# Normalised rows on GpSimd with statistics two slots ahead, and a reworked order in the gates' stage

## The chip, the cores and the metric

One core of one Trainium2 chip runs the whole program. The metric is the device time of one execution in microseconds. Matmuls run on TensorE (PE), element work on VectorE (DVE), ScalarE (ACT) and GpSimd (POOL). All DMAs of this kernel are issued by one queue, SyncE (SP).

## What is computed

For each of 64 graphs with 256 nodes and 256 features, two layers are applied (cut from the reference):

```python
# layer 0
h = max(layernorm(x), 0)
# in the GNN, on h:
x_conv = relu(bn(conv1d(relu(bn(conv1d_1x1(h))), 17 taps)) + h)
s = h @ w_se.T + b_se;  A = exp(-|s_n - s_m|^2) * adj
x_nmp = A @ relu(h @ w_msg.T + b_msg)
gi = concat(x_conv, x_nmp) @ w_ih.T + b_ih;  gh = h @ w_hh.T + b_hh
r = sigmoid(gi_r + gh_r);  z = sigmoid(gi_z + gh_z)
n = tanh(gi_n + r * gh_n)
x = x + (1 - z) * n + z * h
# layer 1
h2 = max(layernorm(x), 0)
x = x + relu(h2 @ W[:d] + (adj @ h2) @ W[d:] + bias)
```

## The kernel before, in words

The program has four stages, one after the other.

1. **Weights** (up to about 77 us): the filters of the long convolution are transformed and split into two f16 halves.
2. **Convolution stage** (about 77 to 390 us), `convolution`. A loop over slots q = 0 to 65 is written out in the program. Slot q has turn(q) (four transposes of the normalised rows xhat), conv1(q-1), forward(q-2) (the transform into frequencies) on PE, and from slot 18 on three chunks of three "main" matmuls each (the products in frequency space). The layer norm of graph f is made in three steps. `layer_stats(f)` takes mean and variance (two `bn_stats` and two `bn_aggr` on DVE, from `xin`). `layer_rstd(f)` makes the root on POOL. `normalise(f)` makes xhat from `xin`, two `tensor_scalar` of 128 x 256 values each, in the kernel before on DVE. xhat and `xin` have two buffers each, by f % 2.
3. **Rest of the main products** (about 390 to 564 us), 60 units of 12 matmuls.
4. **Gates' stage** (about 564 us to the end), `gates`. A slot t has, on each engine, steps of graph t ("cur"), of graph t-1 ("prev") and of graph t+1 ("nxt"), in an order written by hand. Slots 2 to 61 run in a hardware loop of two slots.

Engines synchronise by semaphores only, and each engine does its own instructions strictly in program order, so that a wait holds all that is behind it on its engine. On the SP queue of the convolution stage, slot q issues in this order: `load_x`, `load_adj(q)`, `store_filters(q)` (only in slots 0 to 11), `store_xhat(q)`, `store_h(q)`, then stores of bins and of y. Four waits matter for what follows:

- `load_x(f)` overwrites `xin[f % 2]`, so it waits for `xhat_done` to reach f-1, that is, for normalise(f-2);
- `store_xhat(f)` waits for normalise(f);
- `normalise(f)` overwrites `xhat[f % 2]`, so it waits for turn(f-2) (`turned`) and for store_xhat(f-2) to have landed (`xhat_stored`);
- `turn(f)` on PE waits for normalise(f).

In the gates' stage, `weighted` (PE, into ps_b) is read by `weighted_high` (ACT, L1638) and then `weighted_low` (DVE, L1643), which releases `gates_second(0)` on PE (semaphore `nmp_low`). `gate_sums` (DVE, L1687 and L1690) reads ps_rz and ps_n when `gates_second` is done, and frees ps_n for the next `first_h`. `adj_split_low` is L1578. `finish` (L1817 and L1821) makes the result of a graph from ps_l, which `neighbours` filled.

## Time and profile before

| | |
|---|---|
| median of 3 runs | 1869.83 us (1867.81 to 1880.15) |
| profiled execution | 1870.98 us, of which the span of instructions is 1868.8 us |
| busy share | PE 95%, DVE 80%, ACT 47%, POOL 24% |
| mean granted clock of TensorE | 0.992 of full speed |
| DMA | 245.56 MB, 131 GB/s over the span |

The profiled execution is 1.15 us above the median. Its span is the time from the first to the last instruction, and 2.2 us lie around it. Busy shares are means over stages with different limits, and the rows below are read by stage.

### The profile page before, as it was taken

How to read it: one execution, taken by the hardware profiler on the slowest of the kernel's cores; microseconds unless marked ns; L12 is line 12 of the kernel's file. 1: busy time of each engine (PE TensorE's matmuls, PEld its weight loads, DVE VectorE, ACT ScalarE, POOL GpSimd, SP SyncE). 2: the span in 40 equal slices, each digit the busy share in tenths (PEclk: the TensorE clock that was granted, in tenths of full speed). 3: DMA queues.
4: the chain of work that ended last, by engine and by line, in shares of the span. 5: the costliest groups of instructions: out<-in, count | busy, mean ns of one | idle time of the engine just before them, and what ended most of it. 6: DMA issues, size and time to landing. Idle time of an engine off the chain costs nothing.

```text
span 1868.8 us, 36896 instructions
## 1 busy us (share of the span) xinstructions
PE 1768.8 (95%) x12477; PEld 1167.3 (62%) x12478; DVE 1495.5 (80%) x3322; ACT 875.8 (47%) x1617; POOL 439.2 (24%) x616
## 2 busy tenths in 40 slices
PE   3768999999998999999999999999999999999996
PEld 1456777764445666666666666666666666666664
DVE  4899999962346888888888888888888888888886
ACT  3675555553344444444444444444444444444442
POOL 4511111101012222222222222222222232222221
PEclk9899999999999999999999999999999999999999
DMA  6298887767732322322322322322322322322320
GB/s 201 98 331 261 303 295 270 265 224 250 253 132 94 104 76 81 102 78 80 101 79 80 100 80 79 100 81 78 99 83 76 99 84 75 100 85 74 101 86 17
DMA packets 175187, 245.56 MB, mean 131 GB/s; under 512 B 14781, under 2 KB 111028, under 8 KB 174635
## 3 DMA queue, kind: packets, MB, share of 16 engines
q1 hardware_dynamic: 175128, 244.81, 39.9%
q8 instruction: 33, 0.54, 0.1%
q14 instruction: 26, 0.20, 0.0%
HBM read 154.57 MB, written 90.18 MB: 131 GB/s over the span
## 4 chain that ended last, share of the span: by engine, by line
PE 40%; DVE 21%; ACT 5%; issue 3%; DVEq 0%; POOL 0%; POOLq 0%
PE ps_rz L1551 18%; PE ps_l L1551 13%; PE ps_n L1551 7%; ACT big L1696 3%; ACT big L1591 3%; DVE big L1687 2%; DVE big L1586 2%; DVE big L1621 2%; DVE big L1643 2%; DVE big L1595 2%; DVE big L1578 2%; DVE big L1730 2%; DVE big L1704 2%; PE ps_d L1765 2%; DVE big L1734 2%
## 5 line engine op out<-in xcount | busy, mean ns | idle before, releaser
L1551 PE MATMUL ps_rz<-big 128*128 128x512 f16 x2304 | 560.6, 379 | 13.0 <-DVE big L1643 10.7
L1551 PEld LDWEIGHTS ps_rz<-big 128*128 128x128 f16 x2304 | 220.0, 98 | 224.0 <-DVE big L1643 20.0
L1551 PE MATMUL ps_n<-big 128*128 128x256 f16 x2304 | 314.2, 273 | 0.0
L1551 PEld LDWEIGHTS ps_n<-big 128*128 128x128 f16 x2304 | 225.3, 98 | 94.5
L1551 PE MATMUL ps_l<-big 128*128 128x512 f16 (+1 forms) x1536 | 271.9, 327 | 2.9 <-DVE big L1800 1.5
L1264 PE MATMUL m_ps<-big 128*128 128x512 f16 (+1 forms) x1152 | 268.3, 375 | 3.0 <-DVE big L1029 2.2
L1721 POOL TENSOR_TENSOR big<-big 128x256 f32<-128x256 f32 x128 | 97.5, 762 | 666.9 <-ACT big L1714 666.9
L1696 ACT ACTIVATE big<-big,w_scale 128x512 f32<-128x512 f32 x128 | 92.0, 719 | 283.3 <-DVE big L1687 283.3
L1551 PEld LDWEIGHTS ps_l<-big 128*128 128x128 f16 x1536 | 149.9, 98 | 90.9 <-DVE big L1800 2.0
L1551 PE MATMUL ps_b<-big 128*128 128x256 f16 x1536 | 188.6, 272 | 1.5 <-DVE big L1621 1.5
L1264 PEld LDWEIGHTS m_ps<-big 128*128 128x128 f16 x1152 | 111.8, 98 | 105.1 <-issue 2.2
L1551 PEld LDWEIGHTS ps_b<-big 128*128 128x128 f16 x1536 | 147.0, 98 | 36.3 <-DVE big L1621 19.9
L1034 DVE SCALAR_TENSOR_TENSOR ysb<-m_ps,ysb 128x512 f16<-128x512 f32 x96 | 66.1, 689 | 97.8 <-ACT ysb L926 97.5
L1687 DVE TENSOR_TENSOR big<-ps_rz,w_bias_rz 128x512 f32<-128x512 f32 x128 | 88.8, 693 | 41.5 <-PE ps_rz L1551 36.7
L1714 ACT ACTIVATE big<-big,w_scale 128x256 f32<-128x256 f32 x128 | 65.4, 511 | 92.2 <-DVE big L1707 92.2
L926 ACT ACTIVATE ysb<-m_ps 128x512 f16<-128x512 f32 x96 | 57.0, 594 | 92.5 <-PE m_ps L1264 83.2
L1223 PE MATMUL c_ps<-w1t,front 128*128 128x259 f16 x768 | 97.9, 278 | 0.0
L1817 DVE SCALAR_TENSOR_TENSOR big<-ps_l,w_scale,w_bias_out 128x256 f32<-128x256 f32 x128 | 61.7, 482 | 45.1 <-PE ps_l L1551 45.1
L904 ACT ACTIVATE front<-c 128x512 f16<-128x512 f32 x64 | 40.4, 631 | 121.5 <-DVE c L1017 121.5
L1638 ACT ACTIVATE big<-ps_b 128x512 f16<-128x512 f32 x64 | 38.5, 601 | 124.6 <-PE ps_b L1551 124.6
L1772 ACT ACTIVATE big<-ps_d 128x512 f16<-128x512 f32 x64 | 38.3, 598 | 114.1 <-PE ps_d L1765 114.1
L1521 ACT ACTIVATE big<-ps_s,cvec 128x256 f32<-128x256 f32 x128 | 65.3, 560 | 54.6 <-PE ps_s L1510 54.6
(242 smaller groups left out, 2892.7 us busy)
## 6 DMA issues: line engine op xcount, KB each, us to landing
spectra<-ysb SPq DMA_DIRECT2D x96, 256.0 KB, 2.4
big<-spectra SPq DMA_DIRECT2D x64, 384.0 KB, 3.5
xin<-in_x SPq DMA_DIRECT2D x64, 256.0 KB, 4.0
x_normed<-front SPq DMA_DIRECT2D x64, 256.0 KB, 4.3
h_turned<-front SPq DMA_DIRECT2D x64, 256.0 KB, 3.9
big<-h_turned SPq DMA_DIRECT2D x64, 256.0 KB, 3.2
big<-in_adj SPq DMA_DIRECT2D x64, 256.0 KB, 3.6
big<-in_x SPq DMA_DIRECT2D x64, 256.0 KB, 2.8
```

Source lines behind the costliest of these rows:

```text
L926: act.activation(ysb[:, m % 3, :, 0, :], m_ps[m % 3][:, :].rearrange("p (r o) -> p r o", r=2), ACT.Copy, scale=2.0 ** Y_EXP).then_inc(y_hi ...
L1034: dve.scalar_tensor_tensor(out=ysb[:, m % 3, :, 1, :], in0=m_ps[m % 3][:, :].rearrange("p (r o) -> p r o", r=2), scalar=2.0 ** Y_EXP, in1= ...
L1223: last = pe.matmul(c1_ps[:, t, 0:D + SE], ht[:, f % 2, dl, kh, t * P:t * P + P], w1t[:, wl, kh, 0:D + SE], start=(kh == 0 and n == 0), sto ...
L1264: last = pe.matmul(dest, x_, w_, start=n == 0, stop=n == 11, skip_group_check=True)
L1521: act.activation(conv_y[:, oh, :], ps_s[:, oh * N:oh * N + N], ACT.Identity, scale=cvec[:, 4 + oh:5 + oh], bias=cvec[:, 6 + oh:7 + oh]).th ...
L1551: last = pe.matmul(dest, stationary(dl), moving(wl), start=start and n == 0, stop=stop and n == 2, **kw)
L1591: act.activation(att_s[:, 0, :, :], att[:, :, :], ACT.Copy, scale=w["scale"][:, 6:7]).then_inc(S["att_high"], 1)
L1687: dve.tensor_tensor(sum_rz[:, i, :], ps_rz[i][:, :], w["bias_rz"][:, :], ALU.add).then_inc(S["rz_added"], 1)
L1696: act.activation(tanh_rz[:, i, :], sum_rz[:, i, :], ACT.Tanh, scale=w["scale"][:, 8:9]).then_inc(S["rz_tanh"], 1)
L1714: act.activation(new[:, i, :], pre_n[:, i, :], ACT.Tanh, scale=w["scale"][:, 10:11]).then_inc(S["n_tanh"], 1)
L1721: pool.tensor_tensor(x_new[:, i, :], xin[:, p, i, :], new[:, i, :], ALU.add).then_inc(S["x_new_done"], 1)
L1817: dve.scalar_tensor_tensor(out=out_sum[:, i, :], in0=ps_l[i][:, 0:D], scalar=w["scale"][:, 11:12], in1=w["bias_out"][:, :], op0=ALU.mult, ...
```

## The change

In the convolution stage `normalise` moves from DVE to POOL, behind `layer_rstd` of the same graph. DVE takes the statistics of graph q+2 in slot q, where it took those of q+1, and waits for `xhat_done` before it overwrites `meanvar`. SP loads x one graph earlier: slot q issues `load_x(q+3)` where it issued `load_x(q+2)`, and `load_x(2)` stands ahead of the loop.

In the gates' stage, PE does `neighbours(t-1)` behind `gates_second(t, 1)` where it stood ahead of it. DVE does `gate_sums(t, 1)` at the end of slot t where it was the first step of slot t+1, `weighted_low` ahead of `adj_split_low`, and the result of a graph one slot later, in pieces (`out_row` twice, then `finish`). An extra slot at the end takes the last graph's result.

```diff
@@ SP, convolution stage @@
+                load_x(2)
                 for q in range(SLOTS):
-                    if q + 2 < graphs:
-                        load_x(q + 2)
+                    if q + 3 < graphs:
+                        load_x(q + 3)
@@ POOL, convolution stage @@
-                layer_rstd(0)
-                for q in range(graphs - 1):
-                    layer_rstd(q + 1)
+                def normalise(f):
+                    pool.wait_ge(rstd_done, f + 1)
+                    if f >= 2:
+                        pool.wait_ge(turned, f - 1)
+                        pool.wait_ge(xhat_stored[f % 2], 16 * (f // 2))
+                    for t in range(H):
+                        last = pool.tensor_scalar(xhat[:, f % 2, t, :], xin[:, f % 2, t, :], meanvar[:, f % 2, t, 0:1],
+                                                  rstd[:, f % 2, t:t + 1], ALU.subtract, ALU.mult)
+                    last.then_inc(xhat_done, 1)
+
+                for f in range(graphs):
+                    layer_rstd(f)
+                    normalise(f)
@@ DVE, convolution stage @@
                     dve.wait_ge(x_loaded[f % 2], 16 * (f // 2 + 1))
+                    if f >= 2:
+                        dve.wait_ge(xhat_done, f - 1)
...
                 layer_stats(0)
-                normalise(0)
+                layer_stats(1)
                 for q in range(SLOTS):
-                    if q + 1 < graphs:
-                        layer_stats(q + 1)
+                    if q + 2 < graphs:
+                        layer_stats(q + 2)
...
-                    if q + 1 < graphs:
-                        normalise(q + 1)
@@ gates' stage: new function, and finish without its first step @@
+        def out_row(dve, t, p, i):
+            ready(dve, "out_done", t, i + 1, H)
+            dve.scalar_tensor_tensor(out=out_sum[:, i, :], in0=ps_l[i][:, 0:D], scalar=w["scale"][:, 11:12],
+                                     in1=w["bias_out"][:, :], op0=ALU.mult,
+                                     op1=ALU.add).then_inc(S["out_added"], 1)
@@ SP, gates' stage @@
-                    if prev:
-                        store(sp, t - 1, 1 - p)
+                    if old:
+                        store(sp, t - 2, p)
@@ PE, gates' stage @@
                         first_conv_n(pe, t, p, 1)
+                    if cur:
+                        gates_second(pe, t, p, 1)
                     if prev:
                         neighbours(pe, t - 1, 1 - p)
-                    if cur:
-                        gates_second(pe, t, p, 1)
```

The order of instructions, at the two places that the prediction speaks of. First, the SP queue at the start of the convolution stage (xin<-in_x is `load_x`, wb<-big `store_filters`, x_normed<-front `store_xhat`, h_turned<-front `store_h`). Before:

```order
L692 DMA xin<-in_x 128x2x256 [waits xhat_done]
L740 DMA w_bias_rz<-in_adj 128x512
L712 DMA wb<-big 128x2048
L696 DMA x_normed<-front 128x512 [waits xhat_done]
L700 DMA h_turned<-front 128x1024 [waits h_low]
```

Now:

```order
L692 DMA xin<-in_x 128x2x256 [waits xhat_done] x2
L740 DMA w_bias_rz<-in_adj 128x512
L712 DMA wb<-big 128x2048
L696 DMA x_normed<-front 128x512 [waits xhat_done]
L700 DMA h_turned<-front 128x1024 [waits h_low]
```

One load of x more is issued first, so from here on each load of x in the queue is that of the next graph, and its wait for `xhat_done` asks for one more normalise, ahead of the same stores. On POOL the root was alone (graphs 0 and 1, before):

```order
L813 MEMSET minus_half 128x2
L814 MEMSET eps 128x2
L819 TENSOR_TENSOR rstd<-meanvar,eps 128x2 [waits stats_done,cleared]
L821 TENSOR_TENSOR rstd<-rstd,minus_half 128x2 [waits var_done]
L819 TENSOR_TENSOR rstd<-meanvar,eps 128x2 [waits stats_done]
```

Now (graphs 1 and 2):

```order
L820 TENSOR_TENSOR rstd<-meanvar,eps 128x2 [waits stats_done]
L822 TENSOR_TENSOR rstd<-rstd,minus_half 128x2 [waits var_done]
L831 TENSOR_SCALAR front<-xin,meanvar,rstd 128x256 [waits rstd_done]
L831 TENSOR_SCALAR front<-xin,meanvar,rstd 128x256
L820 TENSOR_TENSOR rstd<-meanvar,eps 128x2 [waits stats_done]
L822 TENSOR_TENSOR rstd<-rstd,minus_half 128x2 [waits var_done]
L831 TENSOR_SCALAR front<-xin,meanvar,rstd 128x256 [waits xhat_stored0,turned,rstd_done]
L831 TENSOR_SCALAR front<-xin,meanvar,rstd 128x256
```

The two normalising instructions and their wait for the store stand on POOL between the roots of neighbouring graphs. Second, DVE in the gates' loop, from the statistics of graph t-1 to `h2_split_low` (L1754 or L1755 is `norm2`). Before:

```order
L1742 BN_AGGR big<-big 128x2
L1578 SCALAR_TENSOR_TENSOR big<-big,w_scale 128x512 [waits g_adj_high]
L1643 SCALAR_TENSOR_TENSOR big<-ps_b,big 128x512 [waits g_nmp_high]
L1754 TENSOR_SCALAR big<-big 128x256 [waits g_turned2,g_rstd2]
L1754 TENSOR_SCALAR big<-big 128x256
L1466 ISA
L1687 TENSOR_TENSOR big<-ps_rz,w_bias_rz 128x512 [waits g_rz_tanh,g_rz_done]
L1690 TENSOR_TENSOR big<-ps_n,w_bias_n 128x512 [waits g_pre_done,g_n_done]
L1777 SCALAR_TENSOR_TENSOR big<-ps_d,big 128x512 [waits g_h2_high]
```

Now:

```order
L1743 BN_AGGR big<-big 128x2
L1814 SCALAR_TENSOR_TENSOR big<-ps_l,w_scale,w_bias_out 128x256 [waits g_out_done]
L1644 SCALAR_TENSOR_TENSOR big<-ps_b,big 128x512 [waits g_nmp_high]
L1755 TENSOR_SCALAR big<-big 128x256 [waits g_turned2,g_rstd2]
L1755 TENSOR_SCALAR big<-big 128x256
L1579 SCALAR_TENSOR_TENSOR big<-big,w_scale 128x512 [waits g_adj_high]
L1814 SCALAR_TENSOR_TENSOR big<-ps_l,w_scale,w_bias_out 128x256 [waits g_out_done]
L1467 ISA
L1688 TENSOR_TENSOR big<-ps_rz,w_bias_rz 128x512 [waits g_rz_tanh,g_rz_done]
L1691 TENSOR_TENSOR big<-ps_n,w_bias_n 128x512 [waits g_pre_done,g_n_done]
L1778 SCALAR_TENSOR_TENSOR big<-ps_d,big 128x512 [waits g_h2_high]
```

The split of adj went behind `weighted_low` and `norm2`, and the two rows of an older graph's result (ps_l) stand among them.

## Rows read from the trace of the kernel before

**Rows 1.** Windows: stretch, length, busy us of PE, PEld, DVE, ACT, POOL, clock, DMA, GB/s

```profile
130.00:140.00 10.00, 6.86 (x62) 5.86 (x61) 9.40 (x27) 7.29 (x16) 1.77 (x4) 1.00 1.01 335
142.24:155.53 13.29, 9.65 (x84) 8.18 (x84) 13.19 (x37) 7.45 (x19) 2.65 (x6) 1.00 0.77 238
200.00:220.00 20.00, 20.00 (x151) 14.86 (x150) 19.86 (x53) 12.05 (x30) 3.53 (x8) 1.00 0.91 316
800.00:1000.00 200.00, 198.45 (x1439) 131.59 (x1438) 167.00 (x361) 89.50 (x160) 51.05 (x60) 1.00 0.27 87
```

**Rows 2.** Timeline, turn on PE in five slots: start, us, engine, line, op

```profile
137.48 0.66 PE L1212 MATMUL turn_ps<-ident,front 128*128 128x128 f32 x4 [1.57 <-DVE front L1001]
142.26 0.66 PE L1212 MATMUL turn_ps<-ident,front 128*128 128x128 f32 x4 [1.57 <-DVE front L1001]
146.70 0.66 PE L1212 MATMUL turn_ps<-ident,front 128*128 128x128 f32 x4 [1.22 <-DVE front L1001]
...
307.71 0.60 PE L1212 MATMUL turn_ps<-ident,front 128*128 128x128 f32 x4
...
312.65 0.60 PE L1212 MATMUL turn_ps<-ident,front 128*128 128x128 f32 x4
```

**Rows 3.** Line L1212 over the run: ns min/median/max, first and last start

```profile
L1212 PE MATMUL turn_ps<-ident,front x256: 272/273/476, 81.0 to 387.2; 128*128 128x128 f32 x128
```

**Rows 4.** Timeline of the SP queue, three issues back to back

```profile
186.43 0.43 SPq L692 DMA_DIRECT2D xin<-in_x  x1
186.90 0.50 SPq L740 DMA_DIRECT2D w_bias_rz<-in_adj  x1
187.45 0.43 SPq L696 DMA_DIRECT2D x_normed<-front  x1
```

**Rows 5.** Line L696, window 185.5 to 190.5: issue to landing of that one store

```profile
DMA to landing us min/median/max: 3.5/3.5/3.5
```

**Rows 6.** Timeline of the SP queue, first slot, with a store of filters between

```profile
80.90 0.37 SPq L692 DMA_DIRECT2D xin<-in_x  x1
...
82.31 0.43 SPq L696 DMA_DIRECT2D x_normed<-front  x1
```

**Rows 7.** Line L696, window 80.5 to 84: landing of that store

```profile
DMA to landing us min/median/max: 4.4/4.4/4.4
```

**Rows 8.** Line L696, all 64 stores of xhat: issue to landing

```profile
DMA to landing us min/median/max: 3.3/4.3/6.4
```

**Rows 9.** Page, DMA issues: KB each, median us to landing

```profile
spectra<-ysb SPq DMA_DIRECT2D x96, 256.0 KB, 2.4
...
xin<-in_x SPq DMA_DIRECT2D x64, 256.0 KB, 4.0
```

**Rows 10.** POOL instructions of the same size: ns min/median/max, first and last start

```profile
L304 POOL TENSOR_SCALAR big<-big,row_scale x10: 920/926/1219, 25.0 to 50.8; 119x256 f32<-119x256 f32 x10
L1721 POOL TENSOR_TENSOR big<-big x128: 637/877/882, 582.0 to 1851.1; 128x256 f32<-128x256 f32 x128
```

**Rows 11.** Timeline of one gates' slot, PE, ACT and DVE

```profile
1011.10 1.47 PE L1551 MATMUL ps_b<-big 128*128 128x256 f16 x12
...
1012.69 0.60 ACT L1638 ACTIVATE big<-ps_b 128x512 f16<-128x512 f32 x1 [1.95 <-PE ps_b L1551]
...
1012.85 0.72 DVE L1578 SCALAR_TENSOR_TENSOR big<-big,w_scale 128x512 f16<-128x512 f32 x1
...
1013.48 0.69 DVE L1643 SCALAR_TENSOR_TENSOR big<-ps_b,big 128x512 f16<-128x512 f32 x1
...
1014.23 1.47 PE L1551 MATMUL ps_rz<-big 128*128 128x512 f16 x6 [0.16 <-DVE big L1643]
...
1017.46 0.69 DVE L1777 SCALAR_TENSOR_TENSOR big<-ps_d,big 128x512 f16<-128x512 f32 x1 [0.37 <-ACT big L1772]
...
1018.58 2.75 PE L1551 MATMUL ps_l<-big 128*128 128x512 f16 x12
```

**Rows 12.** Timeline, the same ps_rz group one slot later

```profile
1034.28 1.47 PE L1551 MATMUL ps_rz<-big 128*128 128x512 f16 x6 [0.15 <-DVE big L1643]
```

More of the change, by code:

```diff
@@ L993, in layer_stats @@
                     last.then_inc(stats_done, 1)
-                def normalise(f):
-                    dve.wait_ge(rstd_done, f + 1)
-                    if f >= 2:
-                        dve.wait_ge(turned, f - 1)
-                        dve.wait_ge(xhat_stored[f % 2], 16 * (f // 2))
-                    for t in range(H):
-                        last = dve.tensor_scalar(xhat[:, f % 2, t, :], xin[:, f % 2, t, :], meanvar[:, f % 2, t, 0:1],
-                                                 rstd[:, f % 2, t:t + 1], ALU.subtract, ALU.mult)
-                    last.then_inc(xhat_done, 1)
                 def split_h(f):
@@ L1815, in finish @@
             for i in range(H):
-                ready(dve, "out_done", t, i + 1, H)
-                dve.scalar_tensor_tensor(out=out_sum[:, i, :], in0=ps_l[i][:, 0:D], scalar=w["scale"][:, 11:12],
-                                         in1=w["bias_out"][:, :], op0=ALU.mult,
-                                         op1=ALU.add).then_inc(S["out_added"], 1)
                 ready(dve, "out_added", t, i + 1, H)
@@ L1825, in slots @@
         def slots(engine, slot):
-            slot(0, 0, False, True, True)
-            slot(1, 1, True, True, True)
+            slot(0, 0, False, False, True, True)
+            slot(1, 1, False, True, True, True)
             with engine.Fori(1, (graphs - 2) // 2) as j:
                 for p in range(2):
-                    slot(j * 2 + p, p, True, True, True)
-            slot(graphs - 2, 0, True, True, True)
-            slot(graphs - 1, 1, True, True, False)
-            slot(graphs, 0, True, False, False)
+                    slot(j * 2 + p, p, True, True, True, True)
+            slot(graphs - 2, 0, True, True, True, True)
+            slot(graphs - 1, 1, True, True, True, False)
+            slot(graphs, 0, True, True, False, False)
+            slot(graphs + 1, 1, True, False, False, False)
         with nc.Block() as block:
@@ L1840, in _, with slot @@
                     sp.wait_ge(early.y_stored[i], 16 * (2 * HALF_UNITS * graphs // GROUP // 3))
-                def slot(t, p, prev, cur, nxt):
+                def slot(t, p, old, prev, cur, nxt):
                     if nxt:
@@ L1859, in _, with slot @@
                 conv_add(pool, 0, 0)
-                def slot(t, p, prev, cur, nxt):
+                def slot(t, p, old, prev, cur, nxt):
                     if prev:
@@ L1876, in _, with slot @@
                 conv_split_high(act, 0, 0)
-                def slot(t, p, prev, cur, nxt):
+                def slot(t, p, old, prev, cur, nxt):
                     if prev:
@@ L1906, in _, with slot @@
                 conv_split_low(dve, 0, 0)
-                def slot(t, p, prev, cur, nxt):
+                def slot(t, p, old, prev, cur, nxt):
                     if prev:
-                        gate_sums(dve, t - 1, 1 - p, 1)
                         gate_new(dve, t - 1, 1 - p, 1)
@@ L1919, in slot @@
                         x1_stats(dve, t - 1, 1 - p, 1)
+                    if old:
+                        out_row(dve, t - 2, p, 0)
                     if cur:
-                        adj_split_low(dve, t, p)
                         weighted_low(dve, t, p)
@@ L1925, in slot @@
                     if cur:
+                        adj_split_low(dve, t, p)
+                    if old:
+                        out_row(dve, t - 2, p, 1)
+                    if cur:
                         gate_sums(dve, t, p, 0)
@@ L1928, in slot @@
                         h2_split_low(dve, t - 1, 1 - p)
+                    if old:
+                        finish(dve, t - 2, p)
                     if cur:
@@ L1936, in slot @@
                         conv_split_low(dve, t + 1, 1 - p)
-                    if prev:
-                        finish(dve, t - 1, 1 - p)
+                    if cur:
+                        gate_sums(dve, t, p, 1)
                 slots(dve, slot)
@@ L1945, in _, with slot @@
                 inverse(pe, 0, 0)
-                def slot(t, p, prev, cur, nxt):
+                def slot(t, p, old, prev, cur, nxt):
                     if cur:
@@ L1967, in slot @@
                         first_conv_n(pe, t, p, 1)
+                    if cur:
+                        gates_second(pe, t, p, 1)
                     if prev:
                         neighbours(pe, t - 1, 1 - p)
-                    if cur:
-                        gates_second(pe, t, p, 1)
                 slots(pe, slot)
```

## The prediction

> **What bounds the kernel now.** I read the windows by stage first, then the timeline of one slot in each stage, then the SP queue. The convolution stage has two limits. In its first 18 slots (no main products yet) DVE is busy 9.40 of 10 us and PE only 6.86 [rows 1], and each turn on PE comes after an idle time of 1.2 to 1.6 us that the normalising instruction on DVE, L1001, ended [rows 2]. A slot takes 142.26 - 137.48 = 4.78 us with a store of filters in it (slots 0 to 11) and 146.70 - 142.26 = 4.44 us without (12 to 17). In the other slots PE is busy 20.00 of 20 us [rows 1] and a slot takes 312.65 - 307.71 = 4.94 us [rows 2]: DVE is nearly as full (19.86) but PE sets the pace. The gates' stage is bound by PE too, 198.45 of 200 us [rows 1], with a slot of 1034.28 - 1014.23 = 20.05 us and one small stall in it, 0.15 to 0.16 us for L1643 on DVE [rows 11, 12].
>
> **The convolution stage: what is removed.** DVE loses two L1001 per slot. In the PE-bound slots that frees an engine that isn't the bound and gives nothing. In the first 18 slots it could give at most the work removed, about 0.73 us of DVE per slot, 18 x 0.73 = 13 us. That is the gain if nothing else comes in its way.
>
> **The convolution stage: the new chain.** Something does. Follow the queue. normalise(q+2) on POOL waits until store_xhat(q) has landed. store_xhat(q) is issued by SP in slot q, behind load_x, and load_x is now that of graph q+3, which waits for normalise(q+1). So the chain is: normalise(q+1) ends, SP issues load_x(q+3), load_adj(q), in slots 0 to 11 store_filters(q), then store_xhat(q); this lands; normalise(q+2) runs. One turn of this ring is one slot. In the kernel before, load_x(q+2) asked only for normalise(q), so store_xhat(q) could go out one normalise earlier and the same ring had two slots of time, about 9.6 to 9.9 us. The store of xhat(q) itself has been ready for a whole slot when SP at last comes to it. Queued behind the waiting load on SP are load_adj, both stores and the stores of bins and y; behind the waiting normalise on POOL is the next root; PE waits for all of it at turn(q+2).
>
> The period of the ring, step by step:
> - POOL's end to SP's issue: 0.05 us, an estimate from L1001's ends and the next L692 in the timeline.
> - From the issue of load_x to that of store_xhat: 187.45 - 186.43 = 1.02 us when the three go out back to back [rows 4], and 82.31 - 80.90 = 1.41 us with a store of filters between [rows 6].
> - Issue to landing of the store: 3.5 us in just that burst [rows 5], 4.4 us in the burst with filters [rows 7]. Over all 64 stores it is 3.3 to 6.4 with median 4.3 us [rows 8]. I take the two bursts, because the ring makes exactly these.
> - Landing to POOL's start: 0.05 us, an estimate of the same kind.
> - normalise on POOL: the trace has no such instruction with two scalar operands. The nearest is L304, a TENSOR_SCALAR with one scalar operand, 119 x 256 f32, median 926 ns; L1721 of 128 x 256 with two tensors takes 637 to 882 ns [rows 10]. I take 2 x 0.93 and 0.14 for the second operation and the gap, 2.0 us. The bounds are 2 x 0.64 + 0.07 = 1.35 and 2 x 1.22 + 0.1 = 2.54 us.
>
> Sum: 0.05 + 1.02 + 3.5 + 0.05 + 2.0 = 6.62 us in a slot without filters, 0.05 + 1.41 + 4.4 + 0.05 + 2.0 = 7.91 us with. Nothing else is later. The load of x(q+2) is issued after normalise(q), lands 4.0 us later [rows 9], and statistics (1.05 us) and root (0.96 us) follow; that is ready before normalise(q+1) has ended one ring later, so it hides. PE's own 4.94 us of work per slot hides in 6.62 as well.
>
> turn(0) starts at 81.0 [rows 3]. normalise(0) takes 1.3 us longer on POOL, so turn(0) moves to about 82.4, and turn(1), behind a root (0.96) and a normalise (2.0) on POOL, comes at about 85.5. Then there are 62 turns of the ring, 12 with filters and 50 without: 12 x 7.91 + 50 x 6.62 = 94.9 + 331.0 = 425.9 us, and turn(63) comes at 511.4 us where the last one starts at 387 now [rows 3]. **This costs +124 us.** What lies behind it in the stage is unchanged.
>
> A rule on the DMA's price can be set beside this. The row shows 3.5 us [rows 5]. The Trainium skill (DMA: Bandwidth & Descriptors, Anatomy of one DMA) gives about 2.0 us fixed and the bytes at 436 GB/s; as an estimate from that page a 256 KB store would land in 2.6 us, the rings would be 5.7 and 6.1 us, and the cost about +75 us. The measured row decides for me; the page's fit leaves out the two loads that share the engines.
>
> **The gates' stage.** L1643 starts at 1013.48, though ACT's half was ready at 1012.69 + 0.60 = 1013.29, because L1578 stands in front of it and runs from 1012.85 [rows 11]. With the split of adj behind it, it can start at about 1013.32, 0.16 us sooner, which is all of PE's stall; ACT sets the end then. 62 slots x 0.16 = 10 us. The out_row in front of it has room: the statistics end 0.5 us before ACT does. gates_second(1) comes 1.3 us earlier on PE than its reader needs, which only adds slack at ps_n, and neighbours needs its input 1.95 us later; at the very end it takes about 1 us off the drain. **-11 us.** What DVE does later in the slot grows by the moved pieces: L1777 ends at 1018.15, while PE starts layer1 at 1018.58 [rows 11], so there is 0.4 us of room, and with out_row and the split of adj (0.48 + 0.72 us) ahead of gate_sums this room is nearly used, since DVE idled about as long there. I cost it at nothing; if it is overrun by 0.2 us, the gain is gone and no more.
>
> **The sum.** 1870.98 + 124 - 11 = 1984 us for the profiled execution, 1983 us against the median.
>
> **Rivals.**
> 1. *The ring holds, at another price* (the forecast's own spread). With the shortest landing of 3.3 us [rows 8] and 1.35 us of POOL the periods are 5.77 and 6.16 us: 74 + 289 = 363 us, 61 us more than now, total about 1922. With the medians that the loaded queue shows (4.3, 4.7 with filters) and 2.54 us of POOL they are 7.96 and 8.75 us: 503 us, total about 2061.
> 2. *The ring does not bind, and the change is faster.* The ring must turn in 4.94 us. With 1.02 us of issues, 1.35 us of POOL and the hops this needs a landing of 2.4 us, which is what a store of y with nothing in front of it takes [rows 9]; with my 2.0 us it needs 1.8. Then DVE's 13 us and the gates' 11 us are gained: 1847 us. Against it: no xhat store of 64 landed under 3.3 us [rows 8], and two loads stand directly in front of it.
> 3. *POOL is held off by DVE.* L1721 of one shape takes 637 ns in some slots and 877 in most [rows 10]. If each normalising instruction meets such an overlap with L1022, the ring grows by 2 x 0.24 us, 62 x 0.48 = 30 us: about 2014 us. If a whole L1022 of 0.69 us blocks each normalise it is 43 us, 2027. The Trainium skill (SBUF — State Buffer, Who interferes with whom) says that a DVE instruction with two SBUF inputs contends with a GpSimd instruction that reads SBUF. By that rule L1022, which reads two SBUF tensors, would be the one to meet here.
> 4. *TensorE's clock falls.* PE would be busy about 4.94 of 6.62 us, 75%. In 142 to 155 us it is busy 9.65 of 13.29 us, 73%, at a granted clock of 1.00 [rows 1], which speaks against it. If it did fall to 1.2 GHz for good, the work of 50 slots would take 9.9 us each: +165 us, about 2150.
>
> **Chances.** The ring at a price between 1930 and 2050 us, rival 3 included: 0.84. Cheaper, 1860 to 1930: 0.05. Dearer or the clock: 0.08. Rival 2: 0.03. A measurement of this kernel can tell about 1%. Faster by over 1% 0.03, within 1% 0.01, slower 0.96. The predicted time is 1983 us, the range 1930 to 2050.
>
> **What the new profile would show.** Right: turns spaced by 6 to 8 us over the whole convolution stage, PE idle before L1212 with POOL's normalise as releaser, POOL waiting for the DMA x_normed<-front, DVE idle too, a gates' slot of 19.9 us. Wrong at the ring: turns still 4.9 us apart. Wrong at a price: the landing of L696 or the mean of the POOL TENSOR_SCALAR off 3.5 us and 1.0 us. Wrong at the gates: a wait of PE for gate_sums or h2_split_low in place of L1643.

## The result and the profile after

The changed kernel takes 2042.24 us (median of 4 runs, 2041.09 to 2045.48), the kernel before 1869.3 us beside it. The ratio is 1.0922 with a 95% interval of 1.0887 to 1.0956: 173 us slower. That is 59 us above the forecast of 1983 us and 8 us inside the upper end of its range. The profiled execution took 2045.48 us with a span of 2043.7 us. The lines of the changed kernel lie a little further down than before: turn on PE is L1213 (L1212 before), the normalising instruction is L831 and now on POOL (L1001 on DVE before), the second half of split_h1 on DVE is L1025 (L1022 before), the four SP issues are L692 (load_x), L740 (load_adj), L712 (store_filters) and L696 (store_xhat) as before.

The loss is in the convolution stage. Line L1213 over the run, on PE alone without its weight loads (instruction durations in ns, first and last start, then what ended PE's idle time before it, in us and times), answers to [rows 3]:

```profile
L1213 PE MATMUL turn_ps<-ident,front x256: 272/273/477, 80.5 to 572.2; 128*128 128x128 f32 x128
its engine sat idle before it (us, times) until:
  POOL front L831: 157.2, 58
```

The last turn starts at 572.2 us where it started at 387.2 before: 185 us later. The windows of one piece of that stage and one of the gates' stage (same columns as [rows 1]):

```profile
100.00:120.00 20.00, 10.72 (x56) 8.02 (x56) 7.92 (x21) 7.26 (x16) 8.11 (x9) 0.74 0.43 158
300.00:350.00 50.00, 36.72 (x240) 24.52 (x238) 29.09 (x73) 18.74 (x43) 23.69 (x26) 0.93 0.51 180
800.00:1000.00 200.00, 200.00 (x1450) 133.09 (x1448) 164.79 (x362) 89.95 (x161) 49.66 (x62) 1.00 0.28 87
```

Around 300 us PE is busy 36.72 of 50 us, DVE 29.09, POOL 23.69 and the DMA engines half: no resource is full. That is what a chain of latencies looks like. In the gates' stage PE is now busy 200.00 of 200 us, 198.45 before [rows 1].

The timeline of POOL, of SP's issues and of turn on PE shows the chain, two turns of it:

```profile
305.58 0.39 SPq L692 DMA_DIRECT2D xin<-in_x  x1
...
306.53 0.43 SPq L696 DMA_DIRECT2D x_normed<-front  x1
...
310.09 2.95 POOL L831 TENSOR_SCALAR front<-xin,meanvar,rstd 128x256 f32<-128x256 f32 x2 [3.58 <-DMA x_normed<-front]
...
313.07 0.39 SPq L692 DMA_DIRECT2D xin<-in_x  x1
...
313.10 0.66 PE L1213 MATMUL turn_ps<-ident,front 128*128 128x128 f32 x4 [0.66 <-POOL front L831]
...
314.02 0.43 SPq L696 DMA_DIRECT2D x_normed<-front  x1
...
317.84 2.76 POOL L831 TENSOR_SCALAR front<-xin,meanvar,rstd 128x256 f32<-128x256 f32 x2 [3.84 <-DMA x_normed<-front]
...
320.63 0.39 SPq L692 DMA_DIRECT2D xin<-in_x  x1
```

Read it as a ring. POOL's normalisation ends at 313.04, SP issues load_x at 313.07 and store_xhat at 314.02, the store lands and POOL starts again at 317.84. From load_x to load_x it is 7.49 and 7.56 us, and PE starts turn 0.06 us after POOL's end (313.10). With a store of filters between, the same timeline reads:

```profile
130.38 0.39 SPq L692 DMA_DIRECT2D xin<-in_x  x1
...
130.40 1.11 PE L1213 MATMUL turn_ps<-ident,front 128*128 128x128 f32 x4 [3.76 <-POOL front L831]
...
131.80 0.43 SPq L696 DMA_DIRECT2D x_normed<-front  x1
...
136.26 2.72 POOL L831 TENSOR_SCALAR front<-xin,meanvar,rstd 128x256 f32<-128x256 f32 x2 [4.96 <-DMA x_normed<-front]
...
139.01 0.39 SPq L692 DMA_DIRECT2D xin<-in_x  x1
```

8.63 us. Over the whole run, first the POOL line, with what it waited for, and then the landing of its stores (this answers to [rows 8]):

```profile
L831 POOL TENSOR_SCALAR front<-xin,meanvar,rstd x128: 1216/1227/1770, 77.9 to 569.1; 128x256 f32<-128x256 f32 x128
its engine sat idle before it (us, times) until:
  DMA x_normed<-front: 260.5, 61
```

```profile
DMA to landing us min/median/max: 3.2/3.6/6.1
```

So 61 of the 62 waits of POOL for the buffer of the store two graphs before are real, 260.5 us in all.

In the gates' stage the timeline of one slot shows what became of the stall of [rows 11]:

```profile
1214.52 0.60 ACT L1639 ACTIVATE big<-ps_b 128x512 f16<-128x512 f32 x1 [2.67 <-PE ps_b L1552]
...
1215.15 0.69 DVE L1644 SCALAR_TENSOR_TENSOR big<-ps_b,big 128x512 f16<-128x512 f32 x1 [0.80 <-ACT big L1639]
...
1215.90 1.47 PE L1552 MATMUL ps_rz<-big 128*128 128x512 f16 x6
```

L1644 now waits for ACT and not for DVE's own queue, and PE has no idle time before ps_rz. Over all slots, the ps_rz line of the page, before and then now (busy us, mean ns, then PE's idle time before it):

```profile
L1551 PE MATMUL ps_rz<-big 128*128 128x512 f16 x2304 | 560.6, 379 | 13.0 <-DVE big L1643 10.7
```

```profile
L1552 PE MATMUL ps_rz<-big 128*128 128x512 f16 x2304 | 560.6, 379 | 1.9 <-DVE big L1545 1.1
```

13.0 us of idle time became 1.9.

### The profile page after: what moved, and what is told of

It reads as the page before. It is cut to its first block, busy times and chain, and to the rows that moved or that the text cites. A ratio compares the mean times of both kernels' runs of the same rounds, so it can differ in the third digit from the quotient of the medians.

```text
span 2043.7 us, 37050 instructions
## 1 busy us (share of the span) xinstructions
PE 1830.8 (90%) x12478; PEld 1196.0 (59%) x12478; DVE 1437.3 (70%) x3194; ACT 879.4 (43%) x1617; POOL 592.8 (29%) x744
## 4 chain that ended last, share of the span: by engine, by line
PE 62%; DVE 1%; ACT 0%; issue 0%; POOL 0%; POOLq 0%; DVEq 0%
PE ps_rz L1552 24%; PE ps_l L1552 12%; PE ps_n L1552 12%; PE ps_b L1552 8%; PE ps_s L1511 3%; PE ps_d L1766 1%; PE ps_d L1561 1%; ACT big L1697 0%; DVE big L1688 0%; DVE big L1705 0%; DVE big L1731 0%; ACT big L1592 0%; DVE big L1587 0%; DVE big L1622 0%; DVE big L1596 0%
## 5 line engine op out<-in xcount | busy, mean ns | idle before, releaser
L1265 PE MATMUL m_ps<-big 128*128 128x512 f16 (+1 forms) x1152 | 277.4, 383 | 1.2 <-DVE ysb L1037 0.6
L1722 POOL TENSOR_TENSOR big<-big 128x256 f32<-128x256 f32 x128 | 105.3, 823 | 590.7 <-ACT big L1715 590.7
L831 POOL TENSOR_SCALAR front<-xin,meanvar,rstd 128x256 f32<-128x256 f32 x128 | 170.4, 1340 | 260.9 <-DMA x_normed<-front 260.5
L1213 PE MATMUL turn_ps<-ident,front 128*128 128x128 f32 x256 | 51.7, 336 | 160.8 <-POOL front L831 157.2
L1002 DVE BATCH_NORM_STATS2 stats<-xin 128x6 f32<-128x256 f32 x128 | 48.1, 418 | 188.6 <-DMA xin<-in_x 188.3
L1213 PEld LDWEIGHTS turn_ps<-ident,front 128*128 128x128 f32 x256 | 33.4, 166 | 186.9 <-POOL front L831 175.5
L1224 PE MATMUL c_ps<-w1t,front 128*128 128x259 f16 x768 | 129.0, 333 | 0.0
L1224 PEld LDWEIGHTS c_ps<-w1t,front 128*128 128x128 f16 x768 | 91.9, 120 | 37.0 <-issue 5.8
L1528 POOL TENSOR_TENSOR big<-big 128x512 f32<-128x512 f32 x64 | 74.3, 1162 | 134.1 <-ACT big L1522 131.4
```

What stands on the lines that cost most here:

```text
L831: last = pool.tensor_scalar(xhat[:, f % 2, t, :], xin[:, f % 2, t, :], meanvar[:, f % 2, t, 0:1], rstd[:, f % 2, t:t + 1], ALU.subtract, A ...
L1002: dve.bn_stats(stats[:, f % 2, t, :], xin[:, f % 2, t, :]).then_inc(stats_raw, 1)
L1213: last = pe.transpose(turn_ps[:, kh * N + t * P:kh * N + t * P + P], xhat[:, f % 2, t, kh * P:kh * P + P], ident[:, :])
L1224: last = pe.matmul(c1_ps[:, t, 0:D + SE], ht[:, f % 2, dl, kh, t * P:t * P + P], w1t[:, wl, kh, 0:D + SE], start=(kh == 0 and n == 0), sto ...
L1265: last = pe.matmul(dest, x_, w_, start=n == 0, stop=n == 11, skip_group_check=True)
L1528: pool.tensor_tensor(conv_x[:, :, :], conv_y[:, :, :], ht[:, p, 0, :, :], ALU.add).then_inc(S["conv_h"], 1)
```

## The experiments

Ten kernels, two of them measured twice. Names: q is the slot, f or q+1, q+2 the graph. Diffs are against the changed kernel if nothing else is said.

### Each part alone

The convolution stage as changed, the gates' stage as before (only the core of the diff; + is this kernel):

```diff
-                    if old:
-                        store(sp, t - 2, p)
+                    if prev:
+                        store(sp, t - 1, 1 - p)
...
+                        gate_sums(dve, t - 1, 1 - p, 1)
...
+                        adj_split_low(dve, t, p)
...
-                        adj_split_low(dve, t, p)
-                    if old:
-                        out_row(dve, t - 2, p, 1)
```

> The convolution stage as changed, the gates' stage as before. Ring theory (each slot of the convolution stage is one turn of: load of x, store of xhat, landing, normalise on GpSimd): the last turn stays at about 572 us and the whole is 10 us above the changed kernel, about 2052 us. A theory in which the gates' reorder costs part of the loss (through a new wait) gives less than 2042 us here.

The gates' stage as changed, the convolution stage as before:

```diff
-                layer_stats(1)
+                normalise(0)
...
-                    if q + 2 < graphs:
-                        layer_stats(q + 2)
+                    if q + 1 < graphs:
+                        layer_stats(q + 1)
...
+                    if q + 1 < graphs:
+                        normalise(q + 1)
```

> The gates' stage as changed, the convolution stage as before. If the reorder removes the 0.16 us stall of each slot and nothing else, 1869 - 10 = 1859 us, with a slot of 19.90 us where it was 20.05. If the stall is only moved to another wait, 1869 us. If the new steps on VectorE hold PE, above 1870.

Measured: the convolution part alone 2052.19 us (ratio 1.0973, 1.0938 to 1.1009), the gates' part alone 1857.91 us (0.9931, 0.9905 to 0.9958). The gates' part takes 2052.19 - 2042.24 = 10.0 us off the one and 1869.8 - 1857.9 = 11.9 off the other (1869.8 is the kernel before, measured beside it). The four runs of the first kernel lie between 2048.3 and 2055.8 us, so within the spread the parts add. Between 800 and 1000 us PE is busy 200.00 of 200 us with the gates' part alone.

What follows: the two parts are independent, the loss is the convolution stage's alone, and the gates' part does what the trace of before promised.

### The ring opened: the store ahead of the load

In SP's order store_xhat(q) is put in front of load_x(q+3), so that it doesn't wait for normalise(q+1). Nothing else changes.

```diff
+                    if q < graphs:
+                        store_xhat(q)
                     if q + 3 < graphs:
                         load_x(q + 3)
...
-                        store_xhat(q)
```

> The changed kernel with one edit: in each slot the SP queue issues store_xhat(q) ahead of load_x(q+3), not behind it. GpSimd still normalises, statistics are still two slots ahead. Ring theory: the store no longer waits for normalise(q+1), the ring has two slots of time again, PE-bound slots go back to 4.94 us and the whole to 1847 to 1862 us. Rival, GpSimd's normalise (2.66 us where VectorE took 0.73) is too slow by itself: the time stays above 2000 us. Rival, TensorE's clock: the same time as the ring theory if its idle time goes, so this run does not tell these two apart.

Measured: 1868.56 us, ratio 0.9988 (0.9971 to 1.0006), 7 us above the range that I had expected. Line L1214 is turn here, on PE alone again:

```profile
L1214 PE MATMUL turn_ps<-ident,front x256: 272/273/448, 81.6 to 395.1; 128*128 128x128 f32 x128
its engine sat idle before it (us, times) until:
...
  POOL front L832: 8.0, 2
```

What follows: POOL ends 8.0 us of PE's waits where it ended 157.2. One issue in another place gives back 2042.24 - 1868.56 = 174 of the 184 us that lie between the changed kernel and the gates' part alone (1857.91 us), with the same slow normalisation on POOL. So nearly the whole loss is the place of the store in SP's queue. It is not quite all: this kernel stays 11 us above the gates' part alone, clear of noise (the intervals 0.9971 to 1.0006 and 0.9905 to 0.9958 don't meet), and POOL still waits 48.3 us in all for stores here. What these 11 us are made of I haven't taken apart.

### The ring opened: a third buffer

The order of SP stays as changed; xhat has three buffers, so that normalise(q+2) waits for store_xhat(q-1), which was issued a whole slot before.

```diff
-                    if f >= 2:
-                        pool.wait_ge(turned, f - 1)
-                        pool.wait_ge(xhat_stored[f % 2], 16 * (f // 2))
+                    if f >= 3:
+                        pool.wait_ge(turned, f - 2)
+                        pool.wait_ge(xhat_stored[f % 3], 16 * (f // 3))
```

> The changed kernel with three buffers of xhat in place of two, SP's order untouched. normalise(q+2) then waits for the landing of store_xhat(q-1), which is one slot older. Ring theory: the ring has two slots and no longer binds; as in the run with the store first, about 1866 us, and 1855 to 1862 if the extra distance also frees the first 18 slots. Rival, SP's order costs by something other than this wait (the queue's other stores held behind the load): above 1900 us.

Measured: 1863.41 us, ratio 0.9967 (0.995 to 0.9985). A second measurement of this kernel, beside others below, gave 1861.36 us; there POOL's line waits 5.3 us in all for stores (260.5 before):

```profile
  DMA x_normed<-front: 4.3, 8
  DMA x_normed<-xhat_c: 1.0, 2
```

What follows: a rival to the ring, that the loads and stores simply take too long for the DMA engines in this order, falls. The landing of the stores is as long as in the changed kernel (median 3.6 us in this second measurement too), it only has time now.

### Each term of the ring

**POOL's duration.** The two normalising instructions back on DVE (0.73 us the pair in place of 2.43 to 2.95), the look-ahead, the loads and SP's order as changed:

```diff
 in the program of DVE
+                    if q + 1 < graphs:
+                        normalise(q + 1)
 in the program of POOL
-                    normalise(f)
```

> The changed kernel with normalise back on VectorE at its old place, statistics and the load of x still one graph further ahead. Theory that the order on SP makes the ring: it still turns once per slot, with VectorE's 0.74 us in place of 2.66: 0.05 + 0.95 + 3.7 + 0.05 + 0.74 = 5.5 us without filters and 6.7 with, about 1910 us; where the next statistics on VectorE wait for x (issued after the same normalise, landing 2.8 us, then 2.7 us of statistics, split and bias ahead of the next normalise) up to 6.5 us per slot and 1965 us. Theory that GpSimd's slow normalise is the loss: with VectorE's normalise the time is that of the gates' part alone, 1858 us.

Measured: 1938.56 us, ratio 1.0352 (1.0321 to 1.0384). Turn goes from 85.4 to 469.7 us, 6.1 us per slot. The theory that POOL's slowness alone makes the loss gave 1858 and is refuted: with DVE's fast instruction the kernel is still 69 us slower than the one before. The ring with DVE would be, from the timings above, 0.95 + 3.5 + 0.73 + 0.1 = 5.3 us, an estimate; the slots take 6.1. The trace of one turn of it:

```profile
304.83 0.43 SPq L696 DMA_DIRECT2D x_normed<-front  x1
...
309.39 0.73 DVE L1003 TENSOR_SCALAR front<-xin,meanvar,rstd 128x256 f32<-128x256 f32 x2
```

The store lands after 3.5 us by the median, 308.3, and DVE comes to its instruction at 309.39 with no idle time before it. What DVE waited for between 80 and 475 us (us in total, times, longest):

```profile
DVE stats L991 <- DMA xin<-in_x: 66.9, 62, 3.3
DVE front L1003 <- DMA x_normed<-front: 15.0, 16, 2.2
```

So the ring of the store is seldom the last to be ready here. What DVE waits for in all 62 slots is the load of x, which SP issues only after the same normalisation: load, statistics, then DVE's other steps, and the next normalisation behind them. It is the second chain that the expectation names. This run refutes the theory of POOL's price alone; it doesn't measure the ring of the store with a fast normalisation.

**The same duration the other way.** A third normalising instruction per graph, into a tile that nothing reads, in front of the two:

```diff
+                    pool.wait_ge(spare_done, f)
+                    pool.tensor_scalar(spare[:, :], xin[:, f % 2, 1, :], meanvar[:, f % 2, 1, 0:1],
+                                       rstd[:, f % 2, 1:2], ALU.subtract, ALU.mult).then_inc(spare_done, 1)
```

> The changed kernel with a third tensor_scalar of 128 x 256 per graph on GpSimd, into a spare tile that nothing reads, between the wait for the store and the two normalising ones. Ring theory: each of 62 turns grows by the instruction's 1.23 to 1.34 us, 76 to 83 us in all, about 2121 us. Rival, GpSimd has slack (it waits 260 us for the store): the instruction hides and the time stays 2042 us.

Measured: 2124.2 us, ratio 1.1356 (1.1324 to 1.1389), 82.0 us over the changed kernel, as expected. In the timeline:

```profile
309.79 1.23 POOL L833 TENSOR_SCALAR spare<-xin,meanvar,rstd 128x256 f32<-128x256 f32 x1 [4.83 <-DMA x_normed<-front]
...
311.00 2.43 POOL L836 TENSOR_SCALAR front<-xin,meanvar,rstd 128x256 f32<-128x256 f32 x2
```

What follows: the extra instruction takes 1.21 us from start to start in this slot and 1.29 us by the mean of all 64, and the time grows by 82.0 / 62 = 1.32 us per turn of the ring. POOL's duration is in the ring at full weight. POOL is busy under half of the time in the changed kernel (23.69 of 50 us), so this is no full engine.

**The issues ahead of the store.** store_xhat(q) directly behind load_x(q+3), ahead of load_adj and the store of filters:

```diff
                     if q + 3 < graphs:
                         load_x(q + 3)
+                    if q < graphs:
+                        store_xhat(q)
...
-                        store_xhat(q)
```

> The changed kernel with store_xhat(q) directly behind load_x(q+3), ahead of load_adj and store_filters. Ring theory: the ring stays but is shorter by the issue of load_adj (0.47 us) and in 12 slots of the filters (0.49 us), and the store lands some 0.3 us sooner with one load less in front of it: 62 x 0.77 + 12 x 1.0 = 60 us less, about 1982 us; at least 62 x 0.47 + 6 = 35 us less, 2007 us. Rival, the ring is not set by the store: no change from 2042 us.

Measured: 1950.09 us, ratio 1.0434 (1.0398 to 1.047). It gave 92 us where I had expected 35 to 60. The rows, POOL's line and then the landing:

```profile
L832 POOL TENSOR_SCALAR front<-xin,meanvar,rstd x128: 1216/1226/1231, 77.2 to 473.9; 128x256 f32<-128x256 f32 x128
its engine sat idle before it (us, times) until:
  DMA x_normed<-front: 166.6, 61
```

```profile
DMA to landing us min/median/max: 2.5/3.1/5.4
```

Three things shrank, of which I had counted one and a half. The issue of the store comes 0.43 us behind load_x and not 0.95 or 1.42: 50 x 0.52 + 12 x 0.99 = 38 us. With one transfer fewer in front of it the store lands sooner. From its issue to POOL's start it is 3.5 us by the mean, where the changed kernel has 4.0 without filters and 4.9 with them: 50 x 0.53 + 12 x 1.39 = 43 us. And no POOL instruction takes over 1231 ns where some took 1770: 2.43 for the pair against a mean of 170.4 / 64 = 2.66 us, 62 x 0.23 = 14 us. The pair still overlaps DVE's split_h1 in most slots, but that one now starts 1.7 to 2.3 us into it (why this matters is said with rival 3 below). Sum 95 us; the two profiled executions differ by 2045.48 - 1948.62 = 97, the medians by 92.

### Is the look-ahead needed at all?

POOL normalises, but statistics and load_x run one slot ahead only, as in the kernel before:

```diff
-                layer_stats(1)
...
-                    if q + 2 < graphs:
-                        layer_stats(q + 2)
+                    if q + 1 < graphs:
+                        layer_stats(q + 1)
...
-                    if q + 3 < graphs:
-                        load_x(q + 3)
+                    if q + 2 < graphs:
+                        load_x(q + 2)
```

> The changed kernel, but statistics and the load of x at their old distance (statistics of q+1 and load of q+2 in slot q); GpSimd normalises. Ring theory: the wait of the load ahead of the store is for normalise(q) again, two slots per ring: slots of 4.94 us in the main part, about 4.6 us in the first 18 (statistics, root, normalise, turn and split now follow each other), the whole 1855 to 1865 us. Rival, GpSimd's normalise is what costs: above 2000 us, since it has even less time here.

Measured: 1901.29 us, ratio 1.0166 (1.0135 to 1.0197). My expectation of 1855 to 1865 us missed by 36 us. The load is issued early enough here, and the ring of the store isn't the bound; another chain is:

```profile
300.67 0.74 DVE L1001 BATCH_NORM_STATS2 stats<-xin 128x6 f32<-128x256 f32 x2
...
301.78 0.20 POOL L819 TENSOR_TENSOR rstd<-meanvar,eps 128x2 f32<-128x2 f32 x1 [2.23 <-DVE meanvar L1004]
...
302.87 2.93 POOL L830 TENSOR_SCALAR front<-xin,meanvar,rstd 128x256 f32<-128x256 f32 x2
...
305.86 0.66 PE L1211 MATMUL turn_ps<-ident,front 128*128 128x128 f32 x4 [0.68 <-POOL front L830]
```

From the statistics to turn it is 305.86 - 300.67 = 5.19 us, all in one slot, and the slot of PE is 4.94 us. PE waits for POOL 56.5 us in all, and POOL for stores only 1.9. That this chain sets the slots is read off the trace; no run here shortens it. Beside the two kernels with the look-ahead and an open ring (1868.6 and 1863.4 us), the look-ahead is worth 33 to 38 us to a kernel that normalises on POOL. The same look-ahead closes the ring when load_x stays ahead of the store in SP's queue. Each half of the change needs something of the other.

### What would the relief of DVE have been worth?

With the ring opened (three buffers) the convolution stage is no faster than before. A cycle of ACT and DVE seemed the cause in the first 18 slots. It can be seen in the kernel with three buffers, by ACT's timeline, with a negation (L949, slots 1 to 11) and without. It negates factors of the convolution's filters, which the first expectation below calls adjacency factors:

```profile
108.72 0.63 ACT L921 ACTIVATE front<-c 128x512 f16<-128x512 f32 x1 [1.35 <-DVE c L1026]
...
110.61 1.06 ACT L949 ACTIVATE big<-big 128x1024 f16<-128x1024 f16 x1
111.56 0.60 ACT L914 ACTIVATE front<-turn_ps 128x512 f16<-128x512 f32 x1
...
113.51 0.63 ACT L921 ACTIVATE front<-c 128x512 f16<-128x512 f32 x1 [1.36 <-DVE c L1026]
...
151.67 0.63 ACT L921 ACTIVATE front<-c 128x512 f16<-128x512 f32 x1 [1.95 <-DVE c L1026]
...
156.11 0.63 ACT L921 ACTIVATE front<-c 128x512 f16<-128x512 f32 x1 [1.95 <-DVE c L1026]
```

4.79 us with, 4.44 us without: the very periods of the kernel before, 4.78 and 4.44 [rows 2], although DVE has 0.73 us less to do. ACT's split_h1 (L921) waits for DVE's add_bias (L1026), which stands behind DVE's split_h, which needs ACT's split_h (L914), which stands behind the negation. Two kernels move the negation from slots 1 to 11 to slots 12 to 22, one with three buffers and POOL's normalisation, one with the gates' part alone (DVE normalises):

```diff
-                    if 1 <= q < HALF_UNITS:
-                        negate(q)
+                    if HALF_UNITS <= q < 2 * HALF_UNITS - 1:
+                        negate(q - HALF_UNITS + 1)
```

> The kernel with three x_hat buffers, with ScalarE's negation of the adjacency factors moved from the units 1 to 11 to the units 12 to 22. In the kernel with three buffers the first 12 units take 4.79 us each, and the next six, which have no negation, 4.44 us. Theory, a cycle of ScalarE and VectorE (split_h, add_bias, split_h1, split_x, adj_sum, negate, split_h of the next unit) sets those units and the negation lies in it: the units 1 to 11 fall to between 4.1 and 4.5 us, the units 12 to 17 rise to about 4.8, and from unit 18 on TensorE hides it. 11 units x 0.35 = 3.9 us won, 5 or 6 x 0.35 = 2 us given back: 1859 to 1862 us, where the same kernel without the move has 1863. Rival, the load of filters or VectorE's own 18 us per 20 us sets them: units of 4.79 us stay and the time is 1863 to 1866.

> The gates' part alone, with ScalarE's negation moved from the units 1 to 11 to the units 12 to 22; the convolution stage normalises on VectorE as before. If the cycle of ScalarE and VectorE sets the first units, the same 0 to 4 us are won: 1854 to 1858 us against 1858 for the gates' part alone. If VectorE's own work sets them (two normalisations more on it, 0.73 us per unit), nothing changes: 1857 to 1860 us. A gain here as large as in the kernel with three buffers says that VectorE's load is not what sets these units.

And the two kernels that they come from, measured again beside them:

> The gates' part alone a second time, beside the two kernels with the moved negation on the same chip: 1858 us, within 3 us of its first measurement (1857.9), so 0.6% under the kernel before.

> The kernel with three x_hat buffers and GpSimd's normalisation a second time, beside the gates' part alone on the same chip. Theory, the normalisation on GpSimd buys nothing even with the ring of the stores taken away, because VectorE was not what set any unit of the convolution stage: the two agree within 6 us (1858 to 1866). Rival, VectorE's relief of 0.73 us per unit shows in the units 0 to 17 once the store is out of the way: 10 us or more under the gates' part alone, 1848 us or less.

| kernel | us (median) | ratio to before (95%) |
|---|---|---|
| gates' part alone, again | 1858.35 | 0.9924 (0.9903 to 0.9946) |
| gates' part, negation later | 1860.85 | 0.9933 (0.9912 to 0.9955) |
| three buffers, again | 1861.36 | 0.9940 (0.9919 to 0.9961) |
| three buffers, negation later | 1865.61 | 0.9977 (0.9960 to 0.9994) |

The moved negation gains nothing in time. Both medians lie above the ranges of the cycle theory (1854 to 1858 and 1859 to 1862 us), and with three buffers the move costs 4 us. 1865.61 lies in the rival's range, but not for the rival's reason, since its slots did change. The periods of the slots did what the cycle says, in turn on PE in the gates' part with the negation later:

```profile
106.62 0.66 PE L1212 MATMUL turn_ps<-ident,front 128*128 128x128 f32 x4 [1.22 <-DVE front L1001]
...
111.05 0.66 PE L1212 MATMUL turn_ps<-ident,front 128*128 128x128 f32 x4 [1.22 <-DVE front L1001]
```

4.43 us, with the store of filters in these slots and with DVE busy 43.19 of 44 us between 106 and 150, where the same slots take 4.79 us with the negation. So the negation sets the difference between 4.79 and 4.44 us; the store of filters doesn't. It is paid back behind. Over the eleven slots from the third turn on this kernel wins 52.68 - 49.34 = 3.3 us on its parent; over the next five, which now have the negation, it loses 23.92 - 22.17 = 1.75 us, and in the slot behind them, which takes 6.79 and not 5.16 us, another 1.6. The six slots behind that lose 30.83 - 29.56 = 1.3 more, though PE bounds them in the parent. In the kernel with three buffers the early slots fell to 4.43 only now and then and came mostly between 4.6 and 5.2, at a DMA share of 0.95 to 0.97. What sets those I haven't separated.

POOL's normalisation buys nothing when nothing stands in its way: 1861.36 against 1858.35 us, intervals overlapping. Turn runs from 80.1 to 386.9 in the one and from 80.6 to 386.7 in the other. In the slots without negation the windows of the two read, DVE's normalisation first and then POOL's:

```profile
140.00:160.00 20.00, 13.55 (x119) 11.49 (x119) 19.86 (x55) 11.29 (x28) 3.94 (x9) 1.00 0.79 246
```

```profile
140.00:160.00 20.00, 15.42 (x124) 11.58 (x124) 17.32 (x47) 11.25 (x26) 14.77 (x19) 1.00 0.70 242
```

DVE falls from 19.86 to 17.32 us of 20, and the slots take 4.43 us in both. In the slots that PE bounds there was nothing to win from the start.

## Why the prediction was right, and where its sizes were off

**The ring: right.** The mechanism came as worked out: turns 7.5 to 8.6 us apart in the rows above, PE waiting for POOL's line, POOL for the store, SP's load directly behind POOL. Two experiments that open it by different means (another order, another buffer) give back 174 and 179 of the 184 us that the convolution part costs, and one that lengthens it by 1.29 us per turn costs 1.32.

**Its price: 61 us too low.** I had put turn(1) at 85.5 and turn(63) at 511.4; they start at 84.9 and 571.9. The mean period is (571.9 - 84.9) / 62 = 7.86 us and not 6.87. By terms, from the timeline of all stores:

- Issue of load_x to issue of store_xhat: 0.95 and 1.42 us against 1.02 and 1.41 predicted. About 4 us less in all.
- The store's landing, issue to POOL's start: mean 4.0 us in the slots without filters (3.4 to 5.5) and 4.9 with them (4.7 without the first, which has two loads in front of it), against 3.55 and 4.45. 49 x 0.45 + 12 x 0.42 = 27 us more. I had taken one burst of each kind for the typical one. The median of 3.6 us agrees with the burst; a sum needs the mean, and of the first 61 stores 18 took 4.5 us or more.
- The normalisation on POOL: mean 170.4 / 64 = 2.66 us the pair against 2.0. 62 x 0.66 = 41 us more, the largest miss. I had taken the instruction with one scalar operand, 926 ns [rows 10]. With two it takes 1227 ns by the median, near the upper end that I had kept (1219, which was the longest of that row).

27 + 41 - 4 = 64 us. The last turn gives back 1.6, since its store has no load in front of it and it takes 5.0 us, and the earlier start 0.6. That makes 62, and the profiled execution is 61 us above the forecast (2045.48 against 1984). **The terms that failed are these two sizes; the step was right.** Both misses went the same way, so that the time lies only 8 us inside the range: the mechanism is confirmed, the price less so.

**Rival 3, POOL held off by DVE, came in part.** What decides is where DVE's L1025 starts. Two slots, the POOL pair of the first being the one at 310.09 above:

```profile
311.34 0.69 DVE L1025 SCALAR_TENSOR_TENSOR front<-c,front 128x512 f16<-128x512 f32 x1 [0.62 <-ACT front L915]
```

```profile
241.78 2.43 POOL L831 TENSOR_SCALAR front<-xin,meanvar,rstd 128x256 f32<-128x256 f32 x2 [3.67 <-DMA x_normed<-front]
...
243.41 0.69 DVE L1025 SCALAR_TENSOR_TENSOR front<-c,front 128x512 f16<-128x512 f32 x1 [0.63 <-ACT front L915]
```

Both times L1025 lies inside the pair. In the first it starts 1.25 us into it, just as the second POOL instruction is due (1.21), and the pair takes 2.95 us. In the second it starts 1.63 us into it and the pair keeps its 2.43. The same pattern runs through all 64 slots. In 35 of them one of the two POOL instructions is due while L1025 runs, or at most 0.12 us before its start, and the pair takes 2.54 to 2.97 us. In 11 L1025 starts 0.15 to 0.26 us after a POOL instruction, and L1025 itself takes 0.82 to 0.94 us while the pair keeps 2.43. In the other 18, 12 of them with an overlap, neither grows. The mean of 2.66 makes 0.23 us per turn, 14 us in all, where I had named 30 to 43. The Trainium skill (SBUF — State Buffer, Who interferes with whom) calls the port that GpSimd shares with VectorE an exclusive lock, and says that a VectorE instruction with two SBUF inputs contends there with a GpSimd instruction that reads SBUF. The trace agrees on which instruction it is, and on POOL's being held back by a running L1025 for most of what is left of it, up to 0.54 us of its 0.69. It differs the other way round: an L1025 that starts 0.4 us or more into a running POOL instruction isn't held back at all.

**The price of the store.** The row of before won over the page's fit, and the measurement is further off still. The Trainium skill (DMA: Bandwidth & Descriptors, Anatomy of one DMA) gives a fit from which 2.6 us is worked out for this store alone, an estimate. The section is about DMAs that GpSimd issues, and this one is issued by SyncE. Here the shortest of 64 takes 3.2 us and the median 3.6, and with one load fewer in front of it the shortest takes 2.5. The prediction's cost by that fit is also summed wrongly: rings of 5.72 and 6.11 us make 50 x 5.72 + 12 x 6.11 = 359 us, which is +58 us on the old stage and not +75.

**Rival 2, and the 13 us of DVE in it: wrong.** This part of my working never came to decide the sum, but it stood there as a gain. Opened, the ring leaves 1861 to 1869 us, not 1847. The step "at most the work removed, 0.73 us of DVE per slot" took DVE's 9.40 of 10 us [rows 1] for the limit. The cycle of ACT and DVE has the same period with 0.73 us less on DVE. That it is this cycle is shown for its one part, the negation, and argued for the rest. The prediction names the slots of 4.78 us by the store of filters; it is the negation in the same slots that makes the difference to 4.44.

**Rival 4, the clock: came, and cost nothing that can be seen.** I had argued that it would stay at 1.00. It was granted at 0.74 between 100 and 120 us and at 0.93 between 300 and 350, means between its two levels of 1.2 GHz (0.5) and 2.4 GHz (1.00), with PE busy 54% and 73% of the time. The row that I had argued from, 73% busy at 1.00 [rows 1], doesn't carry over to a stage with waits of up to 3.8 us (the rows above). Turn takes 1.11 us and not 0.66 in some slots. But PE isn't in the ring: it waits for POOL and no step of the ring waits for it.

**The gates' stage: right in place and size.** -11 us predicted; 10.0, 11.9 and 11.8 us measured (1870.19 - 1858.35 the last). PE's idle time before ps_rz fell by 13.0 - 1.9 = 11.1 us, and the room at L1778, which I had called nearly used, was enough: PE is busy 200.00 of 200 us.

**The best version** is the gates' part alone: 1857.9 and 1858.4 us in two measurements, 0.7 to 0.8% under the kernel before.

## What to carry to other kernels

Ask of every wait that an in-order queue carries out what is queued behind it, and follow it round: a load that is made to wait for one step later also delays the store behind it, and if that store's landing frees the buffer of the next step, the whole chain must fit into one slot instead of two. The remedy costs two swapped lines or one buffer, and the sign of it in a profile is a stage in which no engine and no queue is full. Before moving work off a full engine, look for a cycle through it whose period is the same: here DVE was busy 99% of the time in the slots of 4.43 us, and with 0.73 us per slot taken off it they kept their 4.43 us.

## What the hardware showed that I hadn't expected

- A tensor_scalar of 128 x 256 f32 on POOL with two operands read per partition takes 1227 ns (1216 at least), one with a single such operand of 119 x 256 takes 926 [rows 10]; on DVE the first takes 0.41 us.
- A 256 KB store on SP's queue landed in 3.6 us (median) behind a load of 256 KB and one of the adjacency, and in 3.1 us behind the one load only. So what is issued in the microsecond before a transfer belongs in its estimate.
- TensorE's granted clock was 0.74 between 100 and 120 us, where PE was busy 54% of the time, and 1.00 came back in the gates' stage with PE busy throughout.
- Whether a POOL instruction and DVE's L1025 disturb each other hangs on which starts first and by how much: POOL loses up to 0.54 us, or DVE up to 0.25, or neither loses anything though they overlap.
